# Scatter matmuls in turns with the experts' output products, and the first two groups of experts' input products two and three steps earlier, in a sequence block on one core

## What is computed

```python
q = (xn @ w_q.T).reshape(b, n, 2, h, kd).transpose(2, 0, 1, 3, 4)      # h = 8, kd = 128
sim = jnp.einsum('pbnhd,hkpd->pbnhk', q, keys)                         # 32 keys on either side
s, i = jax.lax.top_k(sim, k)                                           # k = 8
all_scores = (sx[..., :, None] + sy[..., None, :]).reshape(b, n, h, k * k)
scores, pk = jax.lax.top_k(all_scores, k)
idx = jnp.take_along_axis(all_idx, pk, axis=-1)                        # one of 1024 experts
o = jnp.einsum('bnd,bnhkd->bnhk', inputs, key_in[idx])
o = jax.nn.gelu(o, approximate=False) * jax.nn.softmax(scores, axis=-1)
return jnp.einsum('bnhk,bnhkd->bnd', o, key_out[idx])
```

## Time and profile before

| what | value |
|---|---|
| median of 3 runs | 503.56 us (501.24 to 507.07) |
| the profiled execution, its own time | 506.19 us |
| its span, first to last instruction | 504.1 us |
| busy: DVE, PE, ACT, POOL | 86%, 73%, 48%, 46% |
| mean granted TensorE clock | 0.786 |

### The profile page before, as it was taken

How to read it: one execution, slowest core, us unless ns; L and a number is a source line. 1 busy time by engine, 2 the same in 40 slices (tenths; PEclk the granted TensorE clock), 3 DMA queues, 4 the chain that set the end, 5 groups by cost and what they waited for, 6 DMA issues and landing times.

```text
span 504.1 us, 24229 instructions
## 1 busy us (share of the span) xinstructions
PE 366.8 (73%) x10097; PEld 268.3 (53%) x10097; DVE 431.7 (86%) x2755; ACT 243.5 (48%) x398; POOL 232.1 (46%) x311
## 2 busy tenths in 40 slices
PE   5979855166647778786888689768787678878755
PEld 3445543034443557465748474646477347746655
DVE  1557986999999689989999999899999997995923
ACT  2897564355324433574365337443754472445222
POOL 1023350542449344646556474647382925282610
PEclk9979956678656877889797678877987796579769
DMA  8900000000000000000000000000000000000001
GB/s 241 180 1 1 1 1 0 1 1 5 3 5 2 3 4 3 5 3 25 6 1 4 25 5 1 6 25 3 3 6 25 3 3 4 25 3 4 23 5 44
DMA packets 7661, 8.95 MB, mean 18 GB/s; under 512 B 896, under 2 KB 6912, under 8 KB 7424
## 3 DMA queue, kind: packets, MB, share of 16 engines
q1 hardware_dynamic: 6976, 7.34, 5.5%
q10 hardware_dynamic: 576, 0.07, 0.1%
HBM read 5.31 MB, written 2.10 MB: 15 GB/s over the span
## 4 chain that ended last, share of the span: by engine, by line
PE 47%; DVE 17%; issue 14%; POOL 5%; ACT 4%; ACTq 0%; DVEq 0%; POOLq 0%
PE psum L895 17%; PE psum L871 13%; PE psum L882 9%; PE psum L851 6%; DVE idx L623 3%; DVE vals L615 3%; DVE picked L648 2%; DVE arena L679 2%; POOL code L259 2%; POOL arena L286 2%; DVE arena L683 1%; DVE arena L682 1%; DVE arena L676 1%; ACT L434 1%; POOL ixf L254 1%
## 5 line engine op out<-in xcount | busy, mean ns | idle before, releaser
L871 PE MATMUL psum<-arena 64*64 64x16 f16 x8192 | 94.0, 180 | 77.5 <-issue 67.1
L871 PEld LDWEIGHTS psum<-arena 64*64 64x64 f16 x8192 | 86.2, 117 | 94.5 <-issue 85.5
L895 PE MATMUL psum<-ko,arena 64*128 64x128 f32 x1024 | 90.2, 353 | 2.0 <-issue 2.0
L895 PEld LDWEIGHTS psum<-ko,arena 64*128 64x128 f32 x1024 | 86.7, 264 | 2.9 <-issue 2.5
L623 DVE FIND_INDEX8 idx<-vals,sims 128x8 uint32<-128x32 f32 x512 | 82.7, 186 | 0.0
L286 POOL TENSOR_TENSOR arena<-arena 128x512 f32<-128x512 f32 x60 | 77.7, 1328 | 4.3 <-ACT arena L426 4.3
L882 PE MATMUL psum<-x1T,trn 128*64 128x256 f32 x512 | 68.3, 423 | 12.6 <-ACT arena L434 12.6
L679 DVE TENSOR_TENSOR arena<-iota,listsT 128x4096 f16<-128x4096 f16 x32 | 74.9, 2339 | 0.0
L426 ACT ACTIVATE arena<-psum 128x1024 f32<-128x1024 f32 x32 | 32.6, 1018 | 72.5 <-PE psum L871 72.5
L882 PEld LDWEIGHTS psum<-x1T,trn 128*64 128x64 f32 x512 | 36.6, 152 | 51.1 <-ACT arena L434 24.3
L239 POOL TENSOR_TENSOR cand<-vals 128x128 f32<-128x128 f32 x16 | 9.4, 588 | 118.0 <-DVE vals L615 118.0
(11 more groups left out here) (117 smaller groups left out, 563.7 us busy)
## 6 DMA issues: line engine op xcount, KB each, us to landing
x<-in_L_attn_x_dram SPq DMA_DIRECT2D x8, 256.0 KB, 4.8
out_dram<-nat SPq DMA_DIRECT2D x7, 256.0 KB, 2.1
ko<-in_L_ffn_key_out_dram SPq DMA_DIRECT2D x2, 512.0 KB, 9.7
nat<-in_L_ffn_key_in_dram SPq DMA_DIRECT2D x2, 256.0 KB, 9.7
nat<-in_L_ffn_keys_dram SPq DMA_DIRECT2D x2, 128.0 KB, 5.6
out_dram<-nat SPq DMA_DIRECT2D x2, 128.0 KB, 1.7
nat<-in_L_attn_W_delta_dram SPq DMA_DIRECT2D x1, 64.0 KB, 2.8
nat<-in_L_attn_W_in_dram SPq DMA_DIRECT2D x1, 64.0 KB, 2.8
```

The source lines that it names most:

```text
L871: end = pe.matmul(psum[64 * e:64 * e + 64, at:at + NJ], hotx[rows, g, :, e], hotw[rows, part, g, :, e], start=(part == 0), stop=(part == 1))
L895: end = pe.matmul(y2[:, e, m % 2] if m < NS - 1 else y_last[:, e], gl[rows, m % 4, j, :], ko[rows, j, :], start=(j == 0), stop=(j == NJ - 1))
```

## The change

Four edits, all in the order of the work:

- Groups of experts. `experts_in` and `gelus` of groups 0 to 7 stood in steps 1, 3, 5, ... 15; now they stand in steps 0, 1, 5, 7, ... 15 (`GELU_STEP`). Step 3 has none any more.
- Turns. From step 3 on, the first half of a block's scatter and the `experts_out` that followed it are cut up: four rows of scatter (32 matmuls), two parts `j` (8 matmul records), six times; then the last eight rows and the last four parts (`scatter_and_out`). The second half of the last block's scatter is done so too, with the products of block 14.
- The step's beginning. The two `scores` no longer stand together behind the scatter: the first stands after 12 rows, then 10 rows, `lists_turned`, the second, and the last 10 rows. In the last pass `lists_turned` no longer comes first.
- The tail. The second halves of the last two blocks' scatters go to banks 0 and 1, when all similarities are out of them (`p_base`), and wait for one `p_out` less. On POOL, `weigh` of block 13 comes ahead of `halves` of block 15.

```diff
+        def p_base(m, hf):
+
+            return 0 if m * 2 + hf in (2 * NS - 3, 2 * NS - 1) else b_p
+
+        GELU_STEP = (0, 1) + tuple(range(5, NS, 2))
...
             for m in range(NS + 1):
                 if m < NS:
                     candidate_sums(m)
+                if m == NS:
+                    weigh(NS - 3)
                 if m >= 1:
                     halves(m - 1)
-                if m >= 3:
+                if 3 <= m < NS:
                     weigh(m - 3)
...
                     if r == 2:
-                        signs(2 * q + 1)
+                        signs(GELU_STEP[q])
...
-                if m % 2 and m < NS:
-                    gelus(m // 2)
+                if m in GELU_STEP:
+                    gelus(GELU_STEP.index(m))
...
-                if m < NS and m % 2 == 0:
+                if m < NS and m not in GELU_STEP:
                     signs(m)
...
             def scatter(m, hf, first=0, last=32):
-                wait(pe, "p_evac", m * 2 + hf)
-                wait(pe, "hot_done", m * 2 + (hf + 1))
+                if first == 0:
+                    if p_base(m, hf) == 0:
+                        pe.wait_ge(s["sims_ready"], 2 * NS)
+                    wait(pe, "p_evac", m * 2 + hf - (1 if m * 2 + hf > 2 * NS - 4 else 0))
+                    wait(pe, "hot_done", m * 2 + (hf + 1))
...
-                            at = (b_p + tile) * 512 + NJ * k
+                            at = (p_base(m, hf) + tile) * 512 + NJ * k
...
+            def scatter_and_out(m, hf, done):
+                for r in range(8):
+                    scatter(m, hf, 4 * r, 4 * r + 4)
+                    if r < 6:
+                        experts_out(done, 2 * r, 2 * r + 2)
+                experts_out(done, 12, NJ)
 
             scores(0)
             for m in range(NS + 1):
-                if m == NS:
-                    lists_turned(NS - 1)
                 if m >= 2:
                     scatter(m - 2, 1, 0, 12)
-                if 1 <= m < NS:
+                if m + 1 < NS:
+                    scores(m + 1, (0,))
+                if m >= 2:
+                    scatter(m - 2, 1, 12, 22)
+                if m >= 1:
                     lists_turned(m - 1)
+                if m + 1 < NS:
+                    scores(m + 1, (1,))
                 if m >= 2:
-                    scatter(m - 2, 1, 12, 32)
-                if m + 1 < NS:
-                    scores(m + 1)
-                if m % 2 and m < NS:
-                    experts_in(m // 2)
-                if m == NS:
-                    wait(pe, "lists_evac", NS)
-                    experts_out(NS - 3)
-                if m >= 1:
+                    scatter(m - 2, 1, 22, 32)
+                if m in GELU_STEP:
+                    experts_in(GELU_STEP.index(m))
+                if 3 <= m:
+                    wait(pe, "lists_evac", m)
+                    scatter_and_out(m - 1, 0, m - 3)
+                elif m >= 1:
                     scatter(m - 1, 0)
-                if 3 <= m < NS:
-                    wait(pe, "lists_evac", m)
-                    experts_out(m - 3)
-            scatter(NS - 1, 1)
-            experts_out(NS - 2)
+            scatter_and_out(NS - 1, 1, NS - 2)
             experts_out(NS - 1)
```

More of the change, by code:

```diff
@@ L423, in p_out @@
                     wait(act, "a_done", (m - 2) * 4)
-                src = psum[:, b_p * 512:(b_p + 2) * 512].rearrange("p (t g j) -> p j t g", t=2, j=NJ)
+                src = psum[:, p_base(m, hf) * 512:(p_base(m, hf) + 2) * 512].rearrange("p (t g j) -> p j t g", t=2, j=NJ)
                 dst = pn[:, m % 3].rearrange("p j (t g) -> p j t g", t=2)[:, :, :, 32 * hf:32 * hf + 32]
@@ L845, in _, with scores @@
             pe.wait_ge(s["x1T_evac"], NCH)
-            def scores(m):
+            def scores(m, tokens=(0, 1)):
                 wait(pe, "xn_done", m + 1)
-                for t in range(2):
+                for t in tokens:
                     wait(pe, "sims_ready", m * 2 - 1 + t)
@@ L884, in experts_in, with experts_out @@
                     end.then_inc(s["g_mm"], 1)
-            def experts_out(m):
-                wait(pe, "zf_done", m // 2)
-                for j in range(NJ):
+            def experts_out(m, first=0, last=NJ):
+                if first == 0:
+                    wait(pe, "zf_done", m // 2)
+                for j in range(first, last):
                     if m < NS - 1:
@@ L894, in experts_out @@
                         rows = slice(64 * e, 64 * e + 64)
-                        end = pe.matmul(y2[:, e, m % 2] if m < NS - 1 else y_last[:, e], gl[rows, m % 4, j, :], ko[rows, j, :], start=(j == 0),
-                                        stop=(j == NJ - 1))
-                end.then_inc(s["y2_mm"], 1)
+                        end = pe.matmul(y2[:, e, m % 2] if m < NS - 1 else y_last[:, e], gl[rows, m % 4, j, :],
+                                        ko[rows, j, :], start=(j == 0), stop=(j == NJ - 1))
@@ L899, in _ @@
+                if last == NJ:
+                    end.then_inc(s["y2_mm"], 1)
+            def scatter_and_out(m, hf, done):
[4 more added lines that the diff above has]
+                experts_out(done, 12, NJ)
             scores(0)
             for m in range(NS + 1):
-                if m == NS:
-                    lists_turned(NS - 1)
                 if m >= 2:
```

## The result

The changed kernel takes 523.22 us (median of 4 runs, 521.22 to 525.77), the kernel before in the same jobs 505.16 us (501.24 to 507.07): a ratio of 1.037, with a 95% interval of 1.032 to 1.043. It is 18 us slower, where 501.0 us was forecast and the range ended at 508.5.

What follows compares the result with a forecast made beforehand. DVE, busy 86%, and PE, starved by instruction page fetches in the scatter, were taken to hold each other. Terms 3.0 - 6.1 + 1.5 - 1.0 = -2.6 us gave 501.0 us, range 497 to 505, 8 in 10 within 493 to 508.5.

Steps and rivals of the forecast that it cites:

- Rival B: Low clock: 8 turns take 11.5 us, DVE waits 3 us in each of five steps; +9, 510 us; chance 0.14.
- C: Rival: idle goes with the count of scatter matmuls, not pages, so turns save nothing; +14 or so, 515 us; chance 0.04.
- Page stalls: PE's idle "issue" goes down from 67 to some 45 us, in pieces near 1 us.
- Groups in steps 0 and 1: Early steps: waits in step 4 go, -6.1 us; a new wait in step 1, +3.0; net -3.1 us.
- From X to the transposes: Even steps from 6 to 14: transposes end at X + 13.6, DVE waits 1.2 to 1.5 us; net +1.5 us.
- X: The time when PE ends the experts' products of an odd step.
- 11.5 cold: Eight turns at the low clock want 11.5 us, against 7.5 warm and 8.0 from the pages.
- In the odd steps PE waits for DVE's hots and everything has room: Odd steps of the loop: PE waits for DVE's hots, leaving room for everything; no size was given.
- X stays at S + 25.0: Odd steps: POOL sets X, no order of PE's makes it earlier; 25.0 us behind S, 0.9 behind the next.
- S: The start of a step of DVE, at source line L615.
- Tail: After the last X: the last product ends at X + 41.0, gaining 1.0 us; ends -4 and +4.
- shorter stalls: Argument against Rival B: turns have shorter stalls than the 2.49 us of idle at a page's edge.

Runs made afterwards that it cites:

- e4: The kernel before with the loop's turns alone (steps 3 to 15); beginning, groups and tail as before: 499.1 us, ratio 0.992.
- e3: The kernel before with the new groups of experts (GELU_STEP) alone: 500.2 us, ratio 0.996.
- e9: The changed kernel with two unread filler products right ahead of the turns in each even step from 4 on: 514.0 us (507.5 before).
- e10: The changed kernel with 22 rows, transposes, both scores together, then the last 10 rows: 521.0 us, ratio 1.030.
- e13: The changed kernel with 22 rows, transposes, the last 10 rows, then both scores right ahead of the turns: 506.9 us, ratio 1.010.
- e2: The changed kernel with the step's old beginning (12 rows, transposes, 20 rows, both scores), all turns kept: 501.0 us, ratio 0.996.
- e8: The changed kernel with the old beginning and no turns in the tail, new banks and POOL's new order kept: 495.1 us, ratio 0.983.

## Why the prediction was wrong

Rival B, the low clock, is what came; its chance was put at 0.14. By its own terms, +9 on 503.6, its number should have been 512.5; the recorded 510 adds the 9 to the forecast instead (and C's 515 likewise the 14). The low clock isn't the turns' own: e4 has them at 0.786. Step by step:

- *Page stalls.* Right: the turns take them away, and "issue" fell further (17.4 us) than the 45 expected. The rival that had the idle come with the count of scatter matmuls is out, since their count is the same.
- *Groups in steps 0 and 1.* The wait in step 1 was forecast as 3.0 us, due to start at 99.2, and is there with 2.41:

```profile
97.34 1.39 DVE L655 MAX8 picked<-words 128x8 f32<-128x20 f32 x16
101.14 1.39 DVE L655 MAX8 picked<-words 128x8 f32<-128x20 f32 x16 [2.41 <-ACT words L410]
```

  Forecast 3.1 us net, measured alone 2.3 (e3). Right.
- *From X to the transposes.* Right: forecast 13.6 us, in steps 6 to 14 of the changed kernel 12.3 to 14.7, 13.5 on the mean. The block behind X is the one of the odd step, and 8.2 us was put for it where 7.9 to 8.5 were measured. The price at the low clock was too small: "11.5 cold", measured 12.6 to 13.3. It left the scatter of a turn at 0.31 us, but at half clock 80 scatter matmuls take 1.25 us, which makes 0.50 for 32.
- *"In the odd steps PE waits for DVE's hots and everything has room"*, and *"X stays at S + 25.0"*. This is the step that failed. The blocks of the even steps have no term in the prediction. At full clock an even block would have ended about S + 28, by the forecast's own terms; at half clock, behind hots that were late as well, it ended at S + 33 to 35, so PE came late to the odd step. In step 7 the products began at 256.29 and ended at 268.1, S + 29.0:

```profile
256.29 2.60 PE L892 MATMUL psum<-x1T,trn 128*64 128x256 f32 x16
260.94 7.16 PE L892 MATMUL psum<-x1T,trn 128*64 128x256 f32 x48 [2.05 <-ACT arena L441]
```

  POOL's sign was only the floor of X. Over the odd steps 5 to 13 X came at S + 26.7 to 29.3, 27.9 on the mean. And the 25.0 was read from step 7 alone: over the same steps of the kernel before X came at S + 24.1 to 27.6, 26.1 on the mean. The new order also puts ten rows behind the second score, so in step 7 L433 copied P out at 256.42 instead of 251.15, with `sims_out` and the GELUs behind it on ACT. The waits moved into both kinds of steps; here the worst of an even one, and one of an odd one:

```profile
283.20 0.69 DVE L683 TENSOR_TENSOR arena<-iota,listsT 128x1024 f16<-128x1024 f16 x1 [3.18 <-ACT listsT L425]
```
```profile
254.03 0.69 DVE L683 TENSOR_TENSOR arena<-iota,listsT 128x1024 f16<-128x1024 f16 x1 [0.86 <-ACT listsT L425]
```

  In steps 6 to 14 DVE waits 15.5 us for listsT and L410, against 5.9 before and 7.5 forecast. It is also busy 5.0 us longer there (237.3 for 232.4), which no term foresaw and no run explains. DVE's last step began at 469.15 instead of 455.85: 13.3 us lost in the loop, where 1.6 gained were forecast. In e9, with the clock mostly held, it began at 456.06.
- *Tail.* Forecast to end at X + 41.0, 1.0 us sooner than before; the last product ended at X + 51.0. From the start of DVE's last step it is 4.2 us lost (52.5 against 48.3). PE began its turns near the forecast place, X + 19.1 instead of 18.2; from there to the last product's end it took 31.9 us instead of 22.8. The term that was mis-sized is the sixteen turns: the last scatter ended 24.7 us behind their start, against 15.5 by the pages, as both rows of turns ran at half clock.

Why did the argument miss what the rival held? It priced the clock as a mean over the kernel, and weighed "shorter stalls" as a reason for a higher one. What it didn't ask was what stands directly ahead of each block, although the order showed the two scores leave that place in the even steps.

How far such a place goes with the clock, e10 and e13 show: they differ in the place of ten rows of scatter alone, with granted clocks of 0.724 to 0.737 in the four runs of the one and 0.761 to 0.785 in the ten of the other.

## What to carry to other kernels

Interleaving tiny matmuls with larger products did take away most of PE's "issue" idle here (67.1 us before, 17.4 after), but look at every place where such a stretch begins: give it a dense product right ahead, with no wait between, and leave it out where nothing dense can stand there, as in a tail. In e2, e4 and e13 that kept the clock in five even blocks of six each (a granted 0.89 or more), not in all (0.50 in the sixth). A dense piece between two pieces that share banks also covered the copy out of the banks: over steps 4 to 14 PE waited for L433 for 0.4 us in e2 and 5.9 us in e10. When an order is changed for one engine, ask what the moved pieces did for the engine's clock where they stood, not only for the data. A forecast for a loop whose two steps differ needs the clock of each kind of block apart.

## What the runs showed of the hardware

- The same block of turns runs at either clock level, and being busy throughout isn't enough to raise it. In the changed kernel the block of step 10 has PE busy for 13.29 of 13.30 us and yet a granted 0.50, while the same mix of 32 scatter matmuls and 8 products by turns holds 1.00 for 8 us in the odd steps. The level can change within a block, either way: down behind the first turns in e10's step 10 (1.00 from 334.2 to 335.2 us, 0.50 from 336.6 to 346.4, though PE was busy throughout), up behind the first turn in e2's step 10 (0.50 from 323.2 to 324.8, 1.00 from 325.0 to 331.6).
- A switch of shapes between the scatter and the products costs about 0.1 us: turns of 1.02 us at full clock, against 0.31 us of scatter and 0.48 of products on their own, leave 0.2 us for both ways; that is an estimate from these three figures.
- A page of 256 instructions wasn't hidden behind small matmuls. In e8's tail, at half clock, 128 scatter matmuls take 1.9 us and are still followed by 1.7 to 2.2 us of idle:

```profile
471.59 1.90 PE L881 MATMUL psum<-arena 64*64 64x16 f16 x128 [2.20 <-issue]
475.16 1.89 PE L881 MATMUL psum<-arena 64*64 64x16 f16 x128 [1.68 <-issue]
479.18 1.13 PE L881 MATMUL psum<-arena 64*64 64x16 f16 x68 [2.13 <-issue]
```

  From start to start that is 3.6 and 4.0 us at half clock, beside the 3.7 of the earlier trace rows at full clock: in these rows the interval doesn't follow PE's clock. That it is the fetch of a page is an inference from the distance of 256 instructions and the size of the packets, and from the times at which the packets moved: in this stretch of e8 three began, within 472.6 to 472.8, 476.2 to 476.4 and 480.0 to 480.4, each 0.8 to 1.2 us behind the end of a stall.
- The forecast read the pages as one fetched ahead, usable 3.7 us after the one before was entered (3.4 where PE ran freely). The step from 7 to 8 of the kernel before shows the first: from 251.6 to 264.1 us no packet moved, the next began within 264.1 to 264.4, as the scatter behind the products began, and after 142 matmuls of it (284 instructions; by the prediction's count a page begins 285 behind X) PE stood for 1.41 us at "issue". So after 12.5 us without a packet at most one page was ahead. The interval isn't as fixed as the forecast had it: 3.73 us in the earlier trace rows, but here, by its count, about 2.6 (264.3 to 266.97) and 3.3 (266.97 to 270.25, with 0.23 us of idle); the packets began within 268.0 to 268.2 and 271.3 to 271.5.
